# Edge layer of a graph network: GpSimd's 25 gathers of a block issued in five parts, four of them behind a count group of TensorE

## The reference, cut to what matters

```python
x_i = x[dst]; x_j = x[src]
h = relu(concatenate([x_i, x_j - x_i]) @ W1 + b1)
edge_messages = h @ W2 + b2
out = segment_max(edge_messages, dst)
```

## Time and profile before

| | us |
|---|---|
| median of 3 runs | 15991.63 |
| the profiled execution | 16003.64 |
| its span | 16001.9 |
| first to last count eviction of the edge layer | 697.6 to 6808.0 of the span |

### The profile page before, as it was taken

How to read it: one execution, slowest core, us unless ns; L and a number is a source line. 1 busy time by engine, 2 the same in 40 slices (tenths; PEclk the granted TensorE clock), 3 DMA queues, 4 the chain that set the end, 5 groups by cost and what they waited for, 6 DMA issues and landing times. The chain is left out here.

```text
span 16001.9 us, 222885 instructions
## 1 busy us (share of the span) xinstructions
PE 7367.6 (46%) x68791; PEld 5151.8 (32%) x68791; DVE 8618.9 (54%) x11890; ACT 6120.9 (38%) x10705; POOL 7519.5 (47%) x7085
## 2 busy tenths in 40 slices
PE   1155555555555555559979999920000000000055
PEld 1144444444444444425545555510000000000045
DVE  5276766666666766754444434344444444444475
ACT  0133333333333333347767777722222222222201
POOL 4455555555555555431101111166666666666600
PEclk9955555555555555579989989955555555555588
DMA  6333333333333333346646656622222222222186
GB/s 257 141 117 119 121 115 114 114 115 115 115 115 115 115 115 115 104 131 204 204 141 204 200 157 204 183 59 56 55 57 57 58 55 57 57 55 59 47 303 233
DMA packets 1622964, 1983.23 MB, mean 124 GB/s; under 512 B 513958, under 2 KB 1419271, under 8 KB 1617498
## 3 DMA queue, kind: packets, MB, share of 16 engines
q1 hardware_dynamic: 1302057, 1257.39, 26.8%
q10 hardware_dynamic: 94032, 435.46, 6.6%
q0 software_dynamic: 226176, 281.93, 6.3%
HBM read 1171.70 MB, written 816.17 MB: 124 GB/s over the span
## 5 line engine op out<-in xcount | busy, mean ns | idle before, releaser
L644 POOL DMA_INDIRECT RF<-tab_edge_b,idx x3125 | 3417.5, 1094 | 2837.1 <-DMA idx<-e_src 1830.2
L1207 POOL DMA_INDIRECT records<-RF,idx x3125 | 3095.0, 990 | 1591.2 <-issue 990.3
L697 DVE TENSOR_TENSOR HM<-iota_b,eqw 128x2048 bf16<-128x2048 bf16 x2000 | 2193.1, 1097 | 1723.5 <-PE bk L1977 1027.4
L1817 ACT ACTIVATE X<-bk 128x392 uint8<-128x392 f32 x4000 | 1852.5, 495 | 2879.9 <-PE bk L1977 1619.2
L1977 PE MATMUL bk<-HM 128*128 128x98 bf16 x16000 | 1718.5, 267 | 2677.2 <-issue 1547.1
L1977 PE MATMUL kp<-HM,ident_b 128*128 128x98 bf16 x3125 | 275.3, 282 | 4377.2 <-DVEq L1726 2575.9
L1977 PEld LDWEIGHTS bk<-HM 128*128 128x128 bf16 x16000 | 1192.8, 124 | 3199.1 <-issue 3116.0
L781 PE MATMUL tp<-HM,RF 128*64 128x512 bf16 x12276 | 2003.3, 379 | 6.1 <-DVE HM L742 1.1
L881 POOL DMA_INDIRECT agg<-RF,lastT x372 | 528.5, 1421 | 2864.3 <-ACT RF L820 2773.5
L1977 PEld LDWEIGHTS kp<-HM,ident_b 128*128 128x128 bf16 x3125 | 251.7, 141 | 4401.7 <-issue 4401.7
L787 PE MATMUL om<-HM,RF 128*64 128x512 bf16 x6138 | 1451.4, 379 | 0.0
(11 more groups left out here) (375 smaller groups left out, 14032.2 us busy)
## 6 DMA issues: line engine op xcount, KB each, us to landing
dst_f<-counts SPq DMA_DIRECT2D x465, 512.0 KB
RF<-first_rows SPq DMA_DIRECT2D x250, 800.0 KB
counts<-X ACTq DMA_DIRECT2D x250, 784.0 KB
RF<-records SPq DMA_DIRECT2D x220, 784.0 KB, 5.1
records<-pivots SPq DMA_DIRECT2D x120, 1400.0 KB
crow<-counts SPq DMA_DIRECT2D x279, 512.0 KB
first_rows<-RF ACTq DMA_DIRECT2D x25, 4000.0 KB
edge_rows<-RF ACTq DMA_DIRECT2D x125, 800.0 KB
```

Source lines behind the costliest of these rows:

```text
L644: e.indirect_dma_start(out=ring[:, r, j, :], out_offset=None, in_=table[:, :], in_offset=bass.IndirectOffsetOnAxis(ap=idx[:, r, own(j):own ...
L697: return e.tensor_tensor(to[:, 0:n, :].rearrange("p k (q h) -> p k q h", h=2), iota_b[:, 0:m].rearrange("p (q h) -> p q h", h=2).unsqueeze ...
L1207: e.indirect_dma_start(out=records[:, :], out_offset=bass.IndirectOffsetOnAxis(ap=idx2[:, r, j:j + 1], axis=0), in_=msgs[MSG_OF[r]][:, j, ...
L1817: e.activation(staged[u].rearrange("p (r k) -> p r k", k=P)[:, :, k:k + 4], bk[s % 2][:, 0:4 * TILES].rearrange("p (k r) -> p r k", k=4), ...
```

## The change

`gather_slot` issues the 25 gathers in five parts of five. The first part goes out as before. Ahead of the gathers 5, 10, 15 and 20 GpSimd now waits until `banked` has reached group 4, 10, 16 and 22 of the block three before. Blocks 0, 1 and 2, which have no such block, are left as they were. `b` is the block's number, CW is 32.

```diff
         def gather_slot(e, i, r, table):
 
+            b = i * R + r
+
             if isinstance(i, int):
                 e.wait_ge(sem("first_indices"), 16 * R)
             else:
                 wait(e, f"indexed{r}", i * 16)
             gate(e)
             for j in range(K):
+                if j and j % 5 == 0 and not (isinstance(b, int) and b < 3):
+                    wait(e, "banked", b * CW + (j // 5 * 6 - 2 - 3 * CW))
+                    gate(e)
                 e.indirect_dma_start(out=ring[:, r, j, :], out_offset=None, in_=table[:, :],
                                      in_offset=bass.IndirectOffsetOnAxis(ap=idx[:, r, own(j):own(j) + 1], axis=0))\
                     .then_inc(sem(f"moved{r}"), 16)
```

## The result

| | before | changed |
|---|---|---|
| median, same session (4 runs each) | 16002.16 us | 15260.7 us (15237.43 to 15296.35) |
| the profiled execution | 16003.64 | 15296.35 |
| its span | 16001.9 | 15294.3 |
| first to last count eviction | 697.6 to 6808.0 | 638.5 to 6104.8 |

The ratio is 0.9538, 95% interval 0.9516 to 0.956: 4.6% faster, where I had forecast 2.2% slower. The time is not even in the range, which began at 15880. The 707.6 us between the two spans split in three: the edge layer from first to last eviction takes 5466.3 us in place of 6110.4 (644.1 less), it begins 59.1 us earlier, and what follows takes 9189.5 in place of 9193.9.

What follows compares the result with a forecast made beforehand. Waits on the late signal `banked` beside gathers were taken to bound the count part. Per block +4.7, -1.8 and -0.2 make +2.7, x 120 = +324, plus 32 for blocks 0 and 1: +356, forecast 16348 us, range 15880 to 16850.

Steps and rivals of the forecast that it cites:

- Its reading of the wait: Count part beside gathers: TensorE's matmuls ending at 3705.91 were taken as evicted at 3706.94; VectorE stood 10.78 us for that signal.
- the price of a gather in the count part: Count part of each block: every gather there costs 0.90 us, the mean of blocks 116, 61 and 60.
- +4.7: Count part: 20 gathers in place of 14.8, at 0.90 us each, make a block 4.7 us longer.
- The bounds: Whole kernel: 16260 us at 0.77 a gather, 16645 at 1.02 with nothing given back; the case's own range 16150 to 16645.
- The pauses' gift: Count part: three more bursts than before, each pause letting the chain be 0.6 us late before VectorE notices; -1.8 us a block.
- The front: Part of the block ahead of the count part: 12.4 us becomes 12.2 at best, -0.2 us a block.
- Blocks 0 and 1: Start of the edge layer: these blocks, almost free of gathers, get 20 each; +32 us together, each taking over 45 us.
- (a): Rival, count part: each burst pays its late-signal tail and nothing is given back; 17120 us, half of it 16850; chance 0.14.
- (b): Faster rival, count part: VectorE's lead hides bursts, half of the 20 gathers cost 0.3 us; 15836 us, chance 0.18.
- (c): Rival: a gather's place is free, or added gathers only stretch a loss already there; 15990 us, no change; chance 0.08.
- My closing sentence: Count parts under 35 us, or quick handshakes inside a burst, would show the price goes by burst length, not by gather.

Runs made afterwards that it cites:

- the single wait at 5: Changed kernel with only the wait ahead of gather 5 kept, gathers 5 to 24 otherwise without waits: 0.9997 of the kernel before in a 13.7 ms session, 0.9956 in a 16 ms one.

## Why the prediction was wrong

**Right.** That the bound lies in waits of the count part, at the signal `banked`, and not in work: one-hots and evictions kept their length, and all of the 644 us is idle time. That the waits cost GpSimd nothing on the path, its slack just moving. That five groups of gathers would be seen, in part: of the four waits a block 1.8 on the mean made a pause. That 20 gathers would lie in the count part (19.7). A front near 12.2 came out as 12.3 on the mean, by luck: it is 11.5 in four blocks of five and 15.2 in the fifth.

**Its reading of the wait.** That the signal comes late was right, but not by how much: the group that ends at 3705.91 isn't evicted at 3706.94. That is the eviction of the group before it. Its own starts at 3711.89 and ends at 3712.39, 0.14 us before TensorE starts the group two later (3712.53): 6.0 us after its matmuls end, and not 1.0. Read so, the rows of before show the delay growing along the run.

```profile
3711.89 0.50 ACT L1817 ACTIVATE X<-bk 128x392 uint8<-128x392 f32 x1 [4.45 <-remote]
```

**The step that failed** is *the price of a gather in the count part*: "I take the mean of the three blocks, 0.90, since four bursts spread over groups 4 to 26 meet every kind of place, as the 16 do now." The price isn't one of the place. Over blocks 5 to 117 the changed kernel pays (32.0 - 23.1) / 19.7 = 0.45 us for each gather in the count part, where the one before pays (35.4 - 23.1) / 15.6 = 0.79. So 20 x 0.90 against 14.8 x 0.90, +4.7, was in truth 8.9 against 12.3, -3.4. My three blocks, at 0.77, 0.90 and 1.02, were three samples of one condition, a single unbroken run of 25; they could give a price for that alone, and no bound for shorter runs. Where the run stays whole, my step holds: the single wait at 5 made 38.7 us, by 20.8 gathers at 0.75.

**The bounds** failed with it. I took "+4.7" between 0.77 and 1.02, and the range's low end from the faster rival; nothing in it allowed for a price that depends on what went before.

**The pauses' gift.** "-1.8" was reckoned as slack between chain and VectorE. A pause gives far more, since the lag starts low again behind it: in part 4 it is 0.40 us in the first five gathers behind a pause, and was 3.93.

**The front.** I had "-0.2" from block 61 alone, 12.4 against 12.2. The mean front of before was 14.1: in four blocks of five it was 12.6, but 20.6 in the fifth, at the end of a loop pass. Both fell, to 11.5 and 15.2, so the mean by 1.9 us. In a 13.7 ms session the fifth has 16.2 even with no lag, so only a part of the 20.6 was there to gain; what made it up isn't shown.

**Blocks 0 and 1.** "+32" turned out as -59 for the start, and their count parts grew only from 22.4 to 24.9 us (block 0), 14 gathers at 0.18; the two blocks take 40.5 and 42.9 us and not over 45. Here the trace of before had it all: ScalarE stood for 65.23 us ahead of block 0 while gathers went out. I had read the idle time of 76.01 ahead of the gather at 755.96 as proof that block 0 had no gathers beside it, and not asked why block 0 began 17.7 us after the last of them.

**The rivals.** (a), a tail for each burst, had the wrong sign: it took the tail of a long burst for the short ones, beside which the lag is 0.4 to 0.6 us. (b) was the right side with a chance of 0.18 and a break-even of 0.67, which the measured 0.45 passes; its reason, half of the gathers at 0.3 thanks to VectorE's lead, isn't what the lags show, and it gave 15836. (c) had the Trainium skill's rule, "SBUF — State Buffer", "Who interferes with whom", that PE and ACT wait on nobody. In 13.7 ms sessions the rows agree with it: 23.8 us with and without gathers. In 16 ms sessions they don't: 61 us between a transpose and its copy. My closing sentence had named the true rival, a price by the length of the burst; it should have stood among the rivals, with a chance.

**What isn't settled.** Run length orders the lags in each kernel, but isn't all: at 5 to 9 gathers in part 2 the lag is 1.83 us with the single wait and 0.92 in the changed kernel, in different sessions. A pause also thins the gathers out; that it is the break and not the lower rate that helps was to be seen with a wait ahead of each gather, and isn't shown. And whether a gather's issue or its transfer delays a signal of TensorE, and what makes a session one or the other, no run here tells. It is nothing that stays with a chip: the chip numbered 4 in the record gave the 16,513 us and, 55 minutes later, 13,754. The granted clock doesn't explain it: 0.64 in the count part of block 122, 0.62 in the changed block 61's, 0.65 in the 13.7 ms session's; and with the 0.55 of block 61 before, TensorE's work took 18.45 us in place of block 122's 16.83, 1.6 of the 13.7 us by which its count part was longer. Nor is the length counted in gathers alone: ScalarE stood only 1.74 us for its copy at 631.30, deep in a run, before the counts began.

## What to carry to other kernels

A cost beside a long burst must not be priced per item from bursts of one length: look for the same handshake early and late in a burst, and at the longest burst of the program, before moving items about. Where GpSimd issues gathers by the dozen and has slack, spread the slack between them with waits on the consumer's progress and not with timed pauses; that was worth 4.4 to 5.7% in 16 ms sessions and cost nothing in 13.7 ms ones, where short timed pauses cost 2.7 and 2.8%. And time a change of this kind in more than one session, for the loss that it cures may not be there.

## What was unexpected of the hardware

- In a 16 ms session a signal from TensorE reached ScalarE 61 us late beside an unbroken run of gathers on GpSimd, 17 us after its last; in a 13.7 ms session ScalarE's copy at the same place followed after an idle time of 5.63 us, and the mean lag was 0.3 us up to the 25th gather of a run.
- The lag is built up and starts low again behind a pause: 3.93 us on the mean in gathers 20 to 24 of a run, 0.40 in the same part of the slot in the first five behind a pause (changed kernel). Timed pauses of 2.58 us did it; the pause of 1.07 us in block 61 of the changed kernel had been ended by the signal itself, so it doesn't tell how short one may be.
- TensorE's signals were late and ScalarE's weren't: in the same runs of gathers TensorE started 0.14 us, and never over 0.2, after the eviction that it waited for.
- The same kernel took 13.72 to 13.76 ms in four sessions and 15.99 to 16.51 in the others, and the edge layer carried most of it: 4615 us from first to last eviction in a 13.7 ms session with the single wait, 6365 in a 16 ms one.
